# TensorE adds the old membrane and the residual in PSUM, and xh is computed for the new rows of a chunk only

## The reference

```
xn  = groupnorm(x)                      # 32 groups of 8 channels, over the whole image
xh, z = split(xn @ W_in)                # 512 + 512 channels
xc  = depthwise 3x3 convolution of xh   # zero padding
dt_r, B, C = split(xc @ W_xproj)        # 8, 16, 16
dt  = softplus(dt_r @ W_dt + b_dt);  dtN = dt @ W_dtN + b_dtN
for each pixel in order (2304 of an image), 16 states n, 512 channels d:
    h[d,n] = exp(dt[d] * A[n]) * h[d,n] + dtN[n] * B[n] * xc[d]
    y[d]   = sum_n h[d,n] * C[n] + Dskip[d] * xc[d]
y   = layernorm(y) * ln_g + ln_b;  y = y * silu(z)
x   = x + y @ W_out + b_out             # first residual

l   = groupnorm(x) @ W.T + b            # second layer, images taken as time steps
v   = v + (l - v) / 2;  s = (v >= 1);  v = v * (1 - s)
out = x + s                             # second residual
```

## Time and profile before

| | us |
|---|---|
| median of 3 timed runs | 4426.24 (4418.84 to 4433.01) |
| the profiled execution | 4415.12 |
| its span, first to last instruction | 4413.4 |
| VectorE busy | 4047.4 (92%) |
| GpSimd busy | 3843.1 (87%) |
| TensorE busy / weight loads | 3540.8 (80%) / 2225.9 (50%) |
| ScalarE busy | 3411.3 (77%) |
| mean granted TensorE clock | 0.922 of full |

### The profile page before, as it was taken

How to read it: one execution, slowest core, us unless ns; L and a number is a source line. 1 busy time by engine, 2 the same in 40 slices (tenths; PEclk the granted TensorE clock), 3 DMA queues, 4 the chain that set the end, 5 groups by cost and what they waited for, 6 DMA issues and landing times.

```text
span 4413.4 us, 64194 instructions
## 1 busy us (share of the span) xinstructions
PE 3540.8 (80%) x20244; PEld 2225.9 (50%) x20244; DVE 4047.4 (92%) x4017; ACT 3411.3 (77%) x5782; POOL 3843.1 (87%) x2518
## 2 busy tenths in 40 slices
PE   6787888888887788877888778887887788878876
PEld 3454555555555555545554555454554555445544
DVE  3999999999999999999999999999999999999996
ACT  4778787777877787777787777887787777878774
POOL 4999999889998899888999889988899888998894
PEclk8899999998999999999899999999999899999987
DMA  5233223322233223322232223222232223222310
GB/s 132 65 97 100 65 69 100 91 87 62 85 92 92 79 61 103 91 79 75 83 102 73 79 72 101 86 75 76 89 105 65 75 82 105 83 61 80 100 54 22
DMA packets 189295, 363.22 MB, mean 82 GB/s; under 512 B 27416, under 2 KB 164120, under 8 KB 188960
## 3 DMA queue, kind: packets, MB, share of 16 engines
q1 hardware_dynamic: 188960, 359.12, 27.7%
HBM read 289.84 MB, written 69.21 MB: 81 GB/s over the span
## 4 chain that ended last, share of the span: by engine, by line
DVE 26%; ACT 23%; PE 20%; issue 18%; POOL 12%; DVEq 0%; DMA 0%; POOLq 0%; ACTq 0%; SPq 0%
DVE st L1041 18%; POOL st L599 10%; PE ht L1190 8%; ACT decay L727 6%; DVE y L1017 3%; ACT L918 3%; ACT weighed L756 3%; PE work L1227 2%; ACT dt L799 2%; ACT L799 2%; PE work L1262 2%; PE work L1232 1%; PE work L1163 1%; ACT xb L878 1%; PE work L1222 1%
## 5 line engine op out<-in xcount | busy, mean ns | idle before, releaser
L1041 DVE TENSOR_TENSOR_SCAN st<-decay,st 128x1024 f32<-128x1024 f32 (+1 forms) x1536 | 2731.6, 1778 | 138.6 <-ACT decay L727 101.0
L599 POOL TENSOR_TENSOR st<-xc,bbc 128x1536 f32<-128x1536 f32 x768 | 2652.0, 3453 | 56.1 <-DMA bbc<-brow 46.9
L727 ACT ACTIVATE decay<-dt,neg_a 128x1024 f32<-128x1024 f32 (+1 forms) x1536 | 1356.8, 900 | 413.4 <-DVE st L1041 410.7
L1190 PE MATMUL ht<-ident,st 128*128 128x128 f32 x9216 | 1348.5, 297 | 337.1 <-DVE st L1041 299.9
L1190 PEld LDWEIGHTS ht<-ident,st 128*128 128x128 f32 x9216 | 1134.6, 153 | 648.8 <-DVE st L1041 465.1
L1017 DVE SCALAR_TENSOR_TENSOR y<-ht,ct,y 128x512 f32<-128x512 f32 x1536 | 1119.9, 729 | 89.8 <-PE ht L1190 89.4
L632 POOL TENSOR_TENSOR y<-y,weighed 128x512 f32<-128x512 f32 x672 | 854.4, 1271 | 340.3 <-ACT weighed L756 336.1
L756 ACT ACTIVATE weighed<-ht,ct 128x512 f32<-128x512 f32 x672 | 459.4, 684 | 274.1 <-PE ht L1190 271.7
L1227 PE MATMUL work<-xn,win 128*128 128x384 f32 x768 | 344.6, 594 | 136.7 <-DVE volt L997 103.2
L1163 PE MATMUL work<-tri,conv_w 96*32 96x384 f32 x4608 | 415.6, 493 | 5.2 <-issue 2.0
L1222 PE MATMUL work<-xn,win 128*128 128x480 f32 x768 | 359.9, 593 | 4.6 <-ACT xn L850 3.2
(11 more groups left out here) (109 smaller groups left out, 3173.2 us busy)
## 6 DMA issues: line engine op xcount, KB each, us to landing
bbc<-brow SPq DMA_DIRECT2D x192, 768.0 KB, 6.1
tri<-rows_of_xh SPq DMA_DIRECT2D x576, 200.0 KB, 3.9
rows_of_xh<-xhp SPq DMA_DIRECT2D x192, 250.0 KB, 2.4
out_dram<-ot SPq DMA_DIRECT2D x43, 384.0 KB, 4.2
xin<-in_x_dram SPq DMA_DIRECT2D x42, 384.0 KB, 3.4
st<-in_x_dram SPq DMA_DIRECT2D x6, 384.0 KB, 5.5
out_dram<-y SPq DMA_DIRECT2D x4, 384.0 KB, 2.6
brow<-xp SPq DMA_DIRECT2D x48, 24.0 KB, 1.5
```

Of the source, the lines that this page charges most:

```text
L599: u = g.tensor_tensor(slot, xc[:, kq % 2, :, :], bbc[:, piece_slot(kq, p), n % PIECE, :].unsqueeze(1).to_broadcast([P, DC, T]), ALU.mult)
L727: a.activation(flat(decay[:, :, :])[:, lo:hi], flat(dt[:, (k + ahead) % 2, :, :])[:, lo:hi], ACT.Exp, scale=neg_a[:, n:n + 1]).then_inc(s_ ...
L1041: v.tensor_tensor_scan(state[:, lo:hi], flat(decay[:, :, :])[:, lo:hi], state[:, lo:hi], 0.0 if h == 0 else state[:, lo - 1:lo], ALU.mult, ...
L1190: last = t.transpose(ht[:, m, c * P:(c + 1) * P], st[:, j, c, m * P:(m + 1) * P], ident[:, :])
```

## The change

**wo.** A matmul with the identity opens the group: it puts the residual (the tile of `img`) into the bank, and the four matmuls of wo are summed onto it. ScalarE evacuates the bank to `img` with b_out as its bias; VectorE's addition is gone. In the table wo0 stands behind xh0 in step 13, and wo1 moves from step 15 to step 14, behind xh1.

**Membrane.** A matmul with the identity puts `volt` into the bank ahead of the l matmuls. The bias is no longer added before the comparison: VectorE compares with fire_at = unit - b1s (a new tile, computed once an image), and ScalarE adds b1s when it copies the membrane. The reset compares with fire_at too. The charge is gone, at the end of the program too.

**xh.** Only an image's first chunk computes 10 rows; the others compute the 8 new ones, 384 columns. The DRAM buffer holds the 50 rows of an image, a chunk writes its new rows and reads its 10 at their place; the two rows from the chunk before are those that it wrote. The normalisation of the input leaves the upper halo row out.

The core of the diff:

```diff
-    13: ([], [(PRE2, "xh0")], [(POST, "wo0")]),
-    14: ([(PRE, "yi0")], [(PRE2, "xh1")], []),
-    15: ([(PRE, "yi1")], [], [(POST, "wo1")]),
+    13: ([], [(PRE2, "xh0"), (POST, "wo0")], []),
+    14: ([(PRE, "yi0")], [(PRE2, "xh1"), (POST, "wo1")], []),
+    15: ([(PRE, "yi1")], [], []),
...
+        fire_at = sb("fire_at", [P, CH])
...
-        rows_v = nc.dram_tensor("rows_of_xh", [DC, P, (ROWS + 2) * WP], F32).ap()
+        rows_v = nc.dram_tensor("rows_of_xh", [DC, P, (H + 2) * WP], F32).ap()
...
-                sp.dma_start(rows_v[c], xhp[:, c % 3, :, :].rearrange("p r w -> p (r w)")).then_inc(s_put[c], 16)
+                kq = (k + 1) % K
+                r0 = 0 if kq == 0 else TAPS - 1
+                sp.dma_start(rows_v[c][:, (kq * ROWS + r0) * WP:((kq + 1) * ROWS + 2) * WP],
+                             xhp[:, c % 3, r0:, :].rearrange("p r w -> p (r w)")).then_inc(s_put[c], 16)
...
-                                 rows_v[c].rearrange("(g i) e -> i g e", i=Q)[:, :, dy * WP:(dy + ROWS) * WP]
+                                 rows_v[c].rearrange("(g i) e -> i g e", i=Q)[:, :, (top + dy) * WP:(top + dy + ROWS) * WP]
...
-                        a.activation(xhp[:, c % 3, :, 1:1 + W],
-                                     work[:, i, 0:HALO].rearrange("p (r w) -> p r w", w=W),
+                        r0 = 0 if kc == K - 1 else TAPS - 1
+                        a.activation(xhp[:, c % 3, r0:, 1:1 + W],
+                                     work[:, i, 0:HALO - r0 * W].rearrange("p (r w) -> p r w", w=W),
                                      ACT.Copy).then_inc(emptied[i], 1)
...
+                    elif name[:2] == "wo":
+                        h = int(name[2:])
+                        xs = img[:, img_par(b, -1 if k == 0 else 0), h, (k - 1) % K * T:((k - 1) % K + 1) * T]
+                        bank_copy(name, xs, T, func=ACT.Identity, bias=bo[:, h:h + 1])
...
-                    a.activation(volt[:, h, kc * T:(kc + 1) * T], work[:, i, 0:T], ACT.Copy).then_inc(s_kept, 1)
+                    a.activation(volt[:, h, kc * T:(kc + 1) * T], work[:, i, 0:T], ACT.Identity,
+                                 bias=b1s[:, h:h + 1]).then_inc(s_kept, 1)
...
-                    r0, r1 = (W if kx == 0 else 0), (HALO - W if kx == K - 1 else HALO)
+                    r0, r1 = W, (HALO - W if kx == K - 1 else HALO)
...
-                v.scalar_tensor_tensor(out=now, in0=now, scalar=b1s[:, h:h + 1], in1=volt[:, h, cols],
-                                       op0=ALU.add, op1=ALU.add).then_inc(s_volt, 1)
-                dve.wait_ge(s_volt, il + 1)
-                hold("dve", dve, b)
-                v.scalar_tensor_tensor(out=ob[:, h, :], in0=now, scalar=units[:, 1:2],
+                v.scalar_tensor_tensor(out=ob[:, h, :], in0=now, scalar=fire_at[:, h:h + 1],
                                        in1=img[:, img_par(b, -1), h, cols], op0=ALU.is_ge,
                                        op1=ALU.add).then_inc(s_spike, 1)
...
-                    if s in (13, 15) and post:
-
-                        h = (s - 13) // 2
-                        jw = await_filled(dve, b, k, f"wo{h}")
-                        xs = img[:, img_par(b, -1 if k == 0 else 0), h, (k - 1) % K * T:((k - 1) % K + 1) * T]
-                        v.scalar_tensor_tensor(out=xs, in0=work[:, jw, 0:T], scalar=bo[:, h:h + 1],
-                                               in1=xs, op0=ALU.add, op1=ALU.add).then_inc(emptied[jw], 1)
...
+                            v.tensor_scalar(fire_at[:, :], b1s[:, :], -1.0, units[:, 1:2], ALU.mult,
+                                            ALU.add).then_inc(s_b1s, 1)
...
+                            lo = 0 if kc == K - 1 else (TAPS - 1) * W
                             for h in range(CH):
-                                last = t.matmul(work[:, i, 0:HALO], win[:, h, c * P:(c + 1) * P],
-                                                xn[:, (kc + 1) % 3, h, :], start=h == 0, stop=h == CH - 1)
+                                last = t.matmul(work[:, i, 0:HALO - lo], win[:, h, c * P:(c + 1) * P],
+                                                xn[:, (kc + 1) % 3, h, lo:], start=h == 0, stop=h == CH - 1)
...
+                            t.matmul(work[:, i, 0:T], ident[:, :],
+                                     img[:, img_par(b, -1 if k == 0 else 0), h, (k - 1) % K * T:((k - 1) % K + 1) * T],
+                                     start=True, stop=False)
                             for c in range(DC):
                                 pe.wait_ge(s_yz, q0 * DC + c + 1)
                                 last = t.matmul(work[:, i, 0:T], wo[:, c, h * P:(h + 1) * P], zs[:, c, :],
-                                                start=c == 0, stop=c == DC - 1)
+                                                start=False, stop=c == DC - 1)
...
+                            t.matmul(work[:, i, 0:T], ident[:, :], volt[:, h, kc * T:(kc + 1) * T],
+                                     start=True, stop=False)
...
+                t.matmul(ht[:, j % NHT, 0:T], ident[:, :], volt[:, h, kc * T:(kc + 1) * T], start=True, stop=False)
```

More of the change, by code:

```diff
@@ L548, in _ @@
             g.memset(xhp[:, :, :, :], 0.0).then_inc(s_set_pool, 1)
-            g.memset(volt[:, :, :], 0.0)
+            g.memset(volt[:, :, :], 0.0).then_inc(s_set_pool, 1)
             def build_weights():
@@ L969, in group_variance, with fire @@
                 v.tensor_scalar(gn_ve[w][:, :], work[:, i, 0:CH], GN_EPS, None, ALU.add).then_inc(emptied[i], 1)
-            def charge_and_fire(b, k, kc, h):
-                il = ((b - 1) * K + kc) * CH + h
+            def fire(b, k, kc, h):
                 cols = slice(kc * T, (kc + 1) * T)
@@ L996, in reset @@
                 now = work[:, i, 0:T]
-                v.scalar_tensor_tensor(out=volt[:, h, cols], in0=now, scalar=units[:, 1:2], in1=volt[:, h, cols],
+                v.scalar_tensor_tensor(out=volt[:, h, cols], in0=now, scalar=fire_at[:, h:h + 1], in1=volt[:, h, cols],
                                        op0=ALU.is_lt, op1=ALU.mult).then_inc(emptied[i], 1)
@@ L1061, in iteration @@
                                 if a == BOTH_AT and s == a:
-                                    charge_and_fire(b, k, kc, 0)
+                                    fire(b, k, kc, 0)
                                 if a != BOTH_AT and s in (a, a + 1):
-                                    charge_and_fire(b, k, kc, s - a)
+                                    fire(b, k, kc, s - a)
                         if s >= Y_LAG and main:
@@ L1092, in iteration @@
                                 reset(b, k, kc, 0)
-                                charge_and_fire(b, k, kc, 1)
+                                fire(b, k, kc, 1)
                             if a != BOTH_AT and s in (a, a + 1):
@@ L1121, in iteration @@
                                                    in1=b1cs[:, :], op0=ALU.mult, op1=ALU.add).then_inc(emptied[jw], 1)
+                            await_emptied(dve, b, 1, "b1")
+                            v.tensor_scalar(fire_at[:, :], b1s[:, :], -1.0, units[:, 1:2], ALU.mult,
+                                            ALU.add).then_inc(s_b1s, 1)
             walk(dve, iteration)
-            await_emptied(dve, B, 1, "b1")
+            dve.wait_ge(s_b1s, B)
             for j in range(K * CH):
@@ L1127, in _ @@
                 cols = slice(kc * T, (kc + 1) * T)
-                now = ht[:, j % NHT, 0:T]
                 dve.wait_ge(s_end_l, j + 1)
-                v.scalar_tensor_tensor(out=now, in0=now, scalar=b1s[:, h:h + 1], in1=volt[:, h, cols],
-                                       op0=ALU.add, op1=ALU.add).then_inc(s_end_v, 1)
                 need(dve, s_end_t, 2 * (kc - 1))
-                dve.wait_ge(s_end_v, j + 1)
-                v.scalar_tensor_tensor(out=end_spikes(kc, h), in0=now, scalar=units[:, 1:2],
+                v.scalar_tensor_tensor(out=end_spikes(kc, h), in0=ht[:, j % NHT, 0:T], scalar=fire_at[:, h:h + 1],
                                        in1=img[:, img_par(B, -1), h, cols], op0=ALU.is_ge,
@@ L1159, in conv @@
                     pe.wait_ge(s_set_dve, 2)
-                    pe.wait_ge(s_set_pool, 5)
+                    pe.wait_ge(s_set_pool, 6)
                 for dx in range(TAPS):
@@ L1280, in iteration @@
                             pe.wait_ge(s_w1s, b)
+                            if b == 1:
+                                pe.wait_ge(s_set_pool, 5)
+                            else:
+                                await_emptied(pe, b - 1, k, name)
+                            t.matmul(work[:, i, 0:T], ident[:, :], volt[:, h, kc * T:(kc + 1) * T],
+                                     start=True, stop=False)
                             for hi in range(CH):
@@ L1283, in iteration @@
                                                 img[:, img_par(b, -1), hi, kc * T:(kc + 1) * T],
-                                                start=hi == 0, stop=hi == CH - 1)
```

(1 more changed line is left out.)

6 lines of the change are left out of this document (3 added, 3 removed).

## The result

| | before | after |
|---|---|---|
| median, us (4 runs each, side by side) | 4426.87 (4418.84 to 4433.01) | 4450.49 (4449.42 to 4452.02) |
| ratio of the medians, 95% interval | | 1.0055 (1.0037 to 1.0072) |
| the profiled execution / its span | 4415.12 / 4413.4 | 4452.02 / 4450.3 |
| mean granted TensorE clock | 0.922 | 0.922 |

The change makes the kernel 0.55% slower, 24 us by the medians; forecast were 19 us and 4445. The two profiled executions lie 37 us apart, since that of before was a short one.

What follows compares the result with a forecast made beforehand. It took VectorE (92% busy) as the bound, only just, with waits for ScalarE's decay and TensorE's transposes. Terms 31 - 16 - 4 + 8 = +19 us on the median 4426.24 gave 4445 us, range 4395 to 4482.

Steps and rivals of the forecast that it cites:

- Steps 13 to 15, +31: End of each chunk, where wo is added: wo1 ahead of the states of 14 delays VectorE, +31 us over 46 chunks.
- rival A: Faster: TensorE keeps its full clock (2.4 GHz) where it lost it; 4398, 4409 on the median's scale; chance 0.18.
- Membrane, -16: Steps 1, 2 and 9 of chunks with membrane work: VectorE's charges go to TensorE, together -16 us, bounds -55 and +10.
- Step 1: First charged half: two more matmul records at the lower clock, taken as +0.3 us a chunk in 21 chunks.
- step 2: Second charged half: matmuls done long before VectorE asks, so the charge's 0.65 us is won in each of 21 chunks.
- Step 9: Both halves charged together: the first wins nothing, the second 0.65 us 14 times, -9 us; chunk 0 taken as nothing.
- GpSimd, nothing: GpSimd gets nothing new; its y of state 14 comes 1.3 us later, within its lead, so no cost.
- ScalarE, -4: Shorter xh evacuations and input normalisation on ScalarE's path: 40 chunks by 0.1, -4 us, bounds 0 and -12.
- The end, +8: After the last chunk nothing hides TensorE, and six pairs of l groups get identity matmuls: +8 us, bounds 3 and 11.
- Thresholds, nothing: The 8 new threshold instructions sit where VectorE waits for decay: nothing, at most 2 us.
- The rule against it: Judge TensorE by weight loads, optimize the fullest engine: VectorE's whole 110 us saved, 4316 on the median's scale; chance 0.07.

Runs made afterwards that it cites:

- the order alone: The kernel before with only wo1 moved to step 14 ahead of xh1, VectorE adding at that step's end: 4440.19 us, ratio 1.0046.
- xh alone: The kernel before with only the xh part of the change (8 new rows a chunk, halo rows kept in DRAM): 4427.81 us, ratio 1.0017.
- the membrane part alone: The kernel before with only the membrane part of the change: 4408.24 us, ratio 0.9973 to the kernel before.
- both parts and the old wo: The changed kernel with its wo part undone (old table, VectorE's additions, no residual matmul); membrane and xh parts stay: 4414.80 us, ratio 0.9977.
- the best version: The changed kernel with wo1 back in step 15 behind the states of 14, and the last image's l groups as before: 4361.73 us, ratio 0.9872.
- two residual matmuls: The changed kernel with the residual matmul of wo1 done twice: 4473.09 us, ratio 1.0110 to the kernel before.
- the best version with xh as before: The best version, but xh computed with 10 rows and 480 columns as in the kernel before: 4361.40 us, ratio 0.9873.
- wo1 late: The changed kernel with wo1 back in step 15 behind the states of 14, second half's statistics at the next chunk's step 0: 4371.50 us, ratio 0.9880.

## Why the prediction was right

It was right in sign and size, and in the reason for the term that decides; two terms that it had at nothing were not nothing, and they cancel against gains that were larger than forecast (membrane 10 us more, step 4 and GpSimd 14 less). That +24 by the medians lies so near the +19 is in this part luck.

- **Steps 13 to 15, +31.** Measured +31.4, and shown by runs: wo1's place takes it away, a second matmul adds 0.62 us a chunk, ScalarE has no part in it. By kind of chunk it was +0.95 with output transposes (forecast 0.8), +0.5 in an image's last chunk, as forecast, +1.0 in the one before it (forecast 0.5), and -0.3 in the first ones. The one before the last computes xh for the next image's first chunk, with all 480 columns: xh1 takes 1.78 us there against 1.46 elsewhere, and the forecast's sum took 384 columns everywhere. In the first ones the clock stayed full in after (the transposes of 13 took 1.47 us, not the 2.77 of the earlier trace rows), as rival A had it, which gave -0.4 for them.
- **Membrane, -16.** Measured -26, by parts that I had otherwise. Step 1 gave -3.3 (forecast +6), since the clock stayed full in 9 of 21 chunks; step 2 gave -8.0 (forecast -14), for the reset's new wait. Step 9 gave -8.9, the number forecast, but from 17 chunks at 0.57 us less four that gained nothing, where I had 14 at 0.65 and nothing for chunk 0. Step 11 gave another -5.7 that I hadn't, by the clock.
- **Missing: step 4, +8.8.** No instruction is changed there. The clock fell in a wait that was there before, and more often. The membrane part lengthens this wait, from 2.03 us in all 21 chunks to 2.31 (2.5 in 9 of them with that part alone), and every kernel with this part and the old place of the output transposes shows the longer one. The clock fell in 6 of 21 chunks before, in 9 with the order alone and 11 with xh alone, all with the wait at 2.03 us. With the longer wait it is 13 with the membrane part alone, 15 with both parts and the old wo, 15 in the best version, but 10 with two residual matmuls and 10 in the best version with xh as before. So the longer wait goes with more falls; with one trace a kernel and such a spread, what one part adds isn't shown.
- **GpSimd, nothing: wrong.** I wrote that its y of state 14 had more lead than that. The row ahead of the last chunk shows otherwise, after:

```profile
2145.70 1.27 POOL L636 TENSOR_TENSOR y<-y,weighed 128x512 f32<-128x512 f32 x1 [1.74 <-ACT weighed L760]
```

Before, that addition had no wait. ScalarE's weighing comes late since the states do, GpSimd's scan inputs start late, and in the last chunk, where VectorE has little else to do, VectorE's scans wait for GpSimd from scan 5 on instead of from scan 6. Steps 4 to 8 of the last chunks sum to 202.6 us against 197.0. That sum is 199.4 to 204.0 in all kernels with the residual on TensorE, 200.7 with the order alone, and 196.9 to 197.4 in the rest. But it is 201.0 with wo1 late too, where the states of 14 are in time: so the chain read above can't be all of it, and the rest is open.
- **ScalarE, -4:** -2.2 at step 12, the rest can't be told apart. **The end, +8:** +7.6. **Thresholds, nothing:** right, by luck (last section).
- **The rule against it** would have given 4316. VectorE, the fullest engine, lost 91 us of work for a slower kernel, and one more identity matmul of 0.65 us a chunk made it 0.5% slower again. The Trainium skill (Perfetto Trace Analysis, Identifying the Most-Contended Engine) has the engine of highest occupancy optimized first; here the place within TensorE's order decided. The Trainium skill (PSUM — Partial Sum Buffer, Engine vs sequencer instructions) has matmuls start and complete in program order, which is why a place can matter so. The trace agrees: the states of 14 start when yi1 ends, 2496.70, while the scan that they wait for was over at 2492.55, by VectorE's timeline, when the residual had not begun.

## What to carry to other kernels

Moving work from a busy engine to one that also feeds it pays only if it isn't queued ahead of what the first one waits for: lay out the receiving engine's order from its timeline over the tightest stretch, and ask of each moved group what it now stands in front of and what now stands in front of it. With the same matmuls and evacuations this kernel was 0.5% slower with the group ahead of the state transposes and 1.2% faster with it behind them, some of that by a clock that stayed up elsewhere. An estimate of one place is not safe for another: moving a group that waits, as at step 4, handed the wait to the next group, at three times the price.

## What the runs showed of the hardware

The eight new threshold instructions, 256 numbers each, took 1.48 to 1.65 us while GpSimd worked, and 0.23 in the one case in which it didn't. Timeline of VectorE and GpSimd, after:

```profile
2337.34 3.47 POOL L603 TENSOR_TENSOR st<-xc,bbc 128x1536 f32<-128x1536 f32 x1
2339.18 1.65 DVE L1121 TENSOR_SCALAR fire_at<-b1s,units 128x2 f32<-128x2 f32 x1
...
2341.20 2.29 DVE L1046 TENSOR_TENSOR_SCAN st<-decay,st 128x1024 f32<-128x1024 f32 x1 [0.37 <-POOL st L610]
```
```profile
4416.12 0.23 DVE L1121 TENSOR_SCALAR fire_at<-b1s,units 128x2 f32<-128x2 f32 x1
```

VectorE's instruction ends at 2340.83, GpSimd's at 2340.81, and in all seven cases the two ends lie within 0.04 us. So the time booked as VectorE's work was waiting for GpSimd. The Trainium skill (SBUF — State Buffer, SBUF: two separate sides) states this as an exclusive lock on a port pair that the two share. It cost nothing here only because the next scan (state 5 of that chunk) waits for GpSimd anyway: 1.9 us in each of the seven images before, 0.37 after.
